# A fused attention and mixture-of-experts block: own homes for the gathered expert outputs, a new spread of the gathers, and the last expert tile's output products moved into the next unit

## The reference

```python
xn = layernorm(x)                                 # over the 128 channels
# attention: 8 heads of 32, keys and values from a latent of rank 64
q, k, v = heads(xn @ Wq.T), heads(xn @ Wkv_down.T @ Wk_up.T), heads(xn @ Wkv_down.T @ Wv_up.T)
attn = softmax(q k^T / sqrt(32)) v @ Wo.T
# experts: token -> expert floor(xn . wr + br) mod 8
ffn[token] = relu(xn W1[e] + b1[e]) @ W2[e] + b2[e]   # e = expert of the token
out = x + attn + ffn
```

## Time and profile before

| | us |
|---|---|
| median of 3 runs | 505.51 |
| lowest and highest | 501.59 and 506.85 |
| the profiled execution | 505.35 |
| its span in the trace | 503.5 |
| TensorE busy | 456.6 (91%) |
| VectorE busy | 414.5 (82%) |
| GpSimd busy | 376.5 (75%) |

### The profile page before, as it was taken

The page is one execution under the profiler, slowest core; times in us unless marked ns, Lnnn a source line. Parts: engine busy times, 40 slices in busy tenths (PEclk is TensorE's granted clock), DMA queues, the critical chain, the costliest instruction groups (busy, mean ns, idle before and its releaser), DMA issues.

```text
span 503.5 us, 15093 instructions
## 1 busy us (share of the span) xinstructions
PE 456.6 (91%) x4992; PEld 319.7 (63%) x4992; DVE 414.5 (82%) x883; ACT 346.0 (69%) x861; POOL 376.5 (75%) x399
## 2 busy tenths in 40 slices
PE   1868879999999999979999999998999989999967
PEld 1446445665656646658999999964665656656634
DVE  6998988778899899848888888875899898898865
ACT  3686457766777878847777777755766777687654
POOL 4755388888888888717777777757898888988952
PEclk9985899999999999989999999998999999999999
DMA  7994923565573896797878888726474566656322
GB/s 227 331 219 121 270 72 104 125 125 129 145 215 106 204 260 193 224 239 218 262 254 258 262 262 273 227 76 121 89 149 114 132 133 133 129 131 137 84 73 65
DMA packets 82826, 86.74 MB, mean 172 GB/s; under 512 B 10608, under 2 KB 66384, under 8 KB 82768
## 3 DMA queue, kind: packets, MB, share of 16 engines
q1 hardware_dynamic: 78672, 77.60, 57.2%
q0 software_dynamic: 4096, 8.40, 6.7%
HBM read 38.61 MB, written 22.04 MB: 120 GB/s over the span
## 4 chain that ended last, share of the span: by engine, by line
PE 43%; issue 16%; DVE 14%; POOL 13%; DMA 5%; ACT 4%; SPq 3%; POOLq 1%; ACTq 0%; DVEq 0%
POOL padd L592 12%; PE psum L1286 9%; PE psum L1251 8%; PE psum L1270 7%; DVE negm L990 6%; PE psum L1328 4%; PE psum L1301 4%; DMA stk<-mT 4%; SPq L326 3%; PE psum L1199 3%; PE psum L1200 2%; PE psum L1201 2%; DVE split L914 2%; ACT prob L724 2%; PE psum L1220 1%
## 5 line engine op out<-in xcount | busy, mean ns | idle before, releaser
L724 ACT ACTIVATE prob<-psum 128x512 f32<-128x512 f32 x256 | 150.2, 593 | 97.8 <-PE psum L1270 70.4
L990 DVE TENSOR_REDUCE negm<-psum 128x2 f16<-128x512 f32 x256 | 170.6, 682 | 43.3 <-PE psum L1251 36.2
L644 POOL TENSOR_TENSOR padd<-prob 128x512 f32<-128x512 f32 x104 | 126.6, 1218 | 34.6 <-ACT prob L724 26.3
L1251 PE MATMUL psum<-stk 96*128 96x256 f16 x512 | 101.6, 281 | 12.0 <-DVE negm L990 9.4
L592 POOL TENSOR_TENSOR padd<-xTl,padd 128x512 f16<-128x512 f32 x71 | 82.2, 1157 | 36.4 <-DVE padd L1100 36.4
L1270 PE MATMUL psum<-stk 97*128 97x256 f16 x512 | 97.8, 274 | 9.7 <-DMA stk<-mT 4.7
L794 ACT ACTIVATE xTl<-psum,xn_all 128x128 f32<-128x128 f32 x284 | 81.1, 369 | 27.5 <-POOL padd L592 20.7
L610 POOL DMA_INDIRECT xsort<-xn_all,pos x64 | 67.5, 1055 | 14.1 <-issue 13.5
L624 POOL DMA_INDIRECT xn_all<-ysort,pos x64 | 65.4, 1021 | 15.2 <-issue 7.7
L1251 PEld LDWEIGHTS psum<-stk 96*128 96x128 f16 x512 | 41.7, 98 | 54.6 <-DVE negm L990 25.8
L1286 PE MATMUL psum<-prob,vt 128*32 128x256 f32 x1024 | 70.5, 391 | 0.9 <-ACT prob L724 0.8
(11 more groups left out here) (166 smaller groups left out, 882.4 us busy)
## 6 DMA issues: line engine op xcount, KB each, us to landing
stk<-split SPq DMA_DIRECT2D x192, 128.0 KB
xn_all<-wsplit SPq DMA_DIRECT2D x71, 258.0 KB, 4.4
xsort<-oT SPq DMA_DIRECT2D x9, 512.0 KB, 4.9
xTh<-xsort SPq DMA_DIRECT2D x18, 256.0 KB, 4.0
ysort<-xTh SPq DMA_DIRECT2D x18, 256.0 KB, 4.2
out<-acc SPq DMA_DIRECT2D x15, 256.0 KB
acc<-x SPq DMA_DIRECT2D x3, 1024.0 KB, 8.4
xn_all<-W SPq DMA_DIRECT2D x12, 256.0 KB
```

What stands on the lines that cost most here:

```text
L644: nc.gpsimd.tensor_tensor(padd[:, bb, hs], prob[:, bb, hs, 0, :], prob[:, bb, hs, 1, :], ALU.add).then_inc(pool_add, 1)
L724: nc.scalar.activation(prob[:, bb, h, :, :].rearrange("p a c -> p (a c)"), bank[st_bank(u, n)], ACT.Exp, scale=SCALE).then_inc(act_exp, 1)
L990: V.tensor_reduce(negm[:, k % 2, col:col + 2], bank[n % 2].rearrange("p (a c) -> p a c", a=2), AX.X, ALU.max, negate=True).then_inc(dve_ma ...
L1251: ins = mm(bank[n % 2][:, qc * T:(qc + 1) * T], stk[0:96, s, 1, h, t0 + qc * P:t0 + (qc + 1) * P], stk[0:96, s, 0, h, t0:t0 + T], start=Tr ...
```

## The change

- Gathered chunks go to homes of their own, `xn_all[:, j, :]` for chunk j, in place of the two places of `yg`. The wait for `expert_sum(s - 2)` goes; a wait for the landing of the gathers two groups before takes its place.
- The gathers are spread anew: 2 in unit 16 (steps 6 and 7), 4 in each of units 17 to 28 (steps 1, 3, 5, 7), 5 in unit 29 (0, 1, 3, 5, 7), 5 in unit 30 (0, 2, 4, 6, 7) and 4 in unit 31 (1, 3, 5, 6). In units 30 and 31 each waits for `exp` of its step. `expert_sum` stays where it is.
- GpSimd's wait for the stores of `ysort` moves from the start of unit 16 to its step 6, behind the four additions of that unit.
- The last tile's `output(70)` moves into step 2 of unit 16, into bank 5; its `y_out(70)` to VectorE's step 3, ahead of `k_low`; `store_group(17)` into unit 16, behind `load_max(17)`. TensorE enters unit 16 after `y_out(69)`.

```diff
-                for g in range(NT // 4 - 3, NT // 4):
+                for g in range(NT // 4 - 3, NT // 4 - 1):
                     store_group(g)
...
+                    if half == 1 and first and k == 0:
+                        store_group(NT // 4 - 1)
...
-            def gather(s, i):
-                if s >= 2 and i == 0:
-                    pool.wait_ge(dve_out, s - 1)
-                j = 4 * s + i
+            def gather(j):
+
+                g = j // 4
+                if j % 4 == 0 and g >= 2:
+                    pool.wait_ge(pool_g[g % 2], 64 * (g // 2))
                 nc.gpsimd.indirect_dma_start(
-                    out=yg[:, s % 2, i, :], out_offset=None, in_=ysort,
+                    out=xn_all[:, j, :], out_offset=None, in_=ysort,
                     in_offset=bass.IndirectOffsetOnAxis(ap=pos[:, j:j + 1], axis=0)
-                ).then_inc(pool_g[s % 2], 16)
+                ).then_inc(pool_g[g % 2], 16)
+
+            def gathers_at(u):
+
+                return {NU // 2: (6, 7), NU - 3: (0, 1, 3, 5, 7), NU - 2: (0, 2, 4, 6, 7), NU - 1: (1, 3, 5, 6)}.get(u, (1, 3, 5, 7))
...
                 if u == NU // 2:
                     hidden_lows()
-                    for par in range(2):
-                        pool.wait_ge(sp_st[par], 16 * NT // 8)
...
-                    if n % 2 == 1 and u >= NU // 2:
-                        gather(u - NU // 2, n // 2)
+                    if u == NU // 2 and n == 6:
+                        for par in range(2):
+                            pool.wait_ge(sp_st[par], 16 * NT // 8)
+                    if u >= NU // 2 and n in gathers_at(u):
+                        if u >= NU - 2:
+                            pool.wait_ge(act_exp, 8 * u + n + 1)
+                        gather(fetched)
+                        fetched += 1
...
+                        if f and half == 1 and n == 3:
+                            y_out(NTC - 1, 5)
...
+                        if n == 2 and seam:
+                            output(NTC - 1, ex[NTC - 1], 5)
+                        if n == 2 and half == 1 and first and k == 1:
+                            pe.wait_ge(dve_y, NTC)
...
-            output(NTC - 1, ex[NTC - 1])
             pe.wait_ge(dve_kl, u + 3)
             pe.wait_ge(act_h32, NTC - 1)
             proj_k(u + 3, (u + 3) // 2, u + 3)
 
-            pe.wait_ge(dve_y, NTC)
+            pe.wait_ge(dve_y, NTC - 1)
```

More of the change, by code:

```diff
@@ L618, in scatters_at @@
                 return (1, 3, 5, 7) if 11 <= u < 14 else (0, 1, 3, 5, 7)
-            def gather(s, i):
-                if s >= 2 and i == 0:
-                    pool.wait_ge(dve_out, s - 1)
-                j = 4 * s + i
+            def gather(j):
+                g = j // 4
+                if j % 4 == 0 and g >= 2:
+                    pool.wait_ge(pool_g[g % 2], 64 * (g // 2))
                 nc.gpsimd.indirect_dma_start(
-                    out=yg[:, s % 2, i, :], out_offset=None, in_=ysort,
+                    out=xn_all[:, j, :], out_offset=None, in_=ysort,
                     in_offset=bass.IndirectOffsetOnAxis(ap=pos[:, j:j + 1], axis=0)
-                ).then_inc(pool_g[s % 2], 16)
-            sent = 0
+                ).then_inc(pool_g[g % 2], 16)
+            def gathers_at(u):
+                return {NU // 2: (6, 7), NU - 3: (0, 1, 3, 5, 7), NU - 2: (0, 2, 4, 6, 7), NU - 1: (1, 3, 5, 6)}.get(u, (1, 3, 5, 7))
+            sent = fetched = 0
             for u in range(NU):
@@ L1003, in last_experts @@
                 a4 = acc[:, NC - 4:NC, :]
-                V.scalar_tensor_tensor(a4, yg[:, 1, :, :], 1.0 / (WS * WS), a4, ALU.mult, ALU.add
+                V.scalar_tensor_tensor(a4, xn_all[:, NC - 4:NC, :], 1.0 / (WS * WS), a4, ALU.mult, ALU.add
                                        ).then_inc(dve_part, 1)
@@ L1035, in expert_sum @@
                 a4 = acc[:, bass.ds(s * 4, 4), :]
-                V.scalar_tensor_tensor(a4, yg[:, par, :, :], 1.0 / (WS * WS), a4, ALU.mult, ALU.add
+                V.scalar_tensor_tensor(a4, xn_all[:, bass.ds(s * 4, 4), :], 1.0 / (WS * WS), a4, ALU.mult, ALU.add
                                        ).then_inc(dve_out, 1)
@@ L1100, in hid_high, with y_out @@
                 V.tensor_copy(hh[:, t % 4, :], h32[:, t % 2, :]).then_inc(dve_hh, 1)
-            def y_out(t):
+            def y_out(t, b=None):
                 dve.wait_ge(pe_y, t + 1)
@@ L1105, in y_out @@
                     dve.wait_ge(sp_st[t // 4 % 2], t // 8 * 16)
-                V.reduce_sum(ys[:, t % 8, :], bank[2 + t % 2][:, 0:2 * D].rearrange("p (a d) -> p d a", a=2), AX.X
+                V.reduce_sum(ys[:, t % 8, :], bank[b or 2 + t % 2][:, 0:2 * D].rearrange("p (a d) -> p d a", a=2), AX.X
                              ).then_inc(dve_y, 1)
@@ L1175, in _ @@
                     y_out(t - 2)
-            for i in range(2):
-                row_max(NU // 2 + 1, LEAD - 8 + i, NU // 2 + 1)
-                y_out(NTC - 2 + i)
+            row_max(NU // 2 + 1, LEAD - 8, NU // 2 + 1)
+            y_out(NTC - 2)
+            row_max(NU // 2 + 1, LEAD - 7, NU // 2 + 1)
             body(NIT // 2, 1, True, False)
@@ L1194, in _ @@
             mm = nc.tensor.matmul
+            ex = []
             pe.wait_ge(pool_const, 4)
@@ L1395, in hidden, with output @@
                 ins.then_inc(pe_h, 1)
-            def output(t, e):
+            def output(t, e, b=None):
                 pe.wait_ge(pool_hl, t + 1)
@@ L1402, in output @@
                 k = t % 4
-                dst = bank[2 + t % 2]
+                dst = bank[b or 2 + t % 2]
                 for fc in range(FC):
@@ L1469, in _ @@
             hidden(0)
-            ex = []
             for t in range(NTC):
```

1 line of the change is left out of this document (removed).

## The result

The changed kernel takes 522.44 us in the median of 6 runs (520.31 to 526.18); beside it the kernel before took 505.31 (501.59 to 506.85). The ratio is 1.0344, with a 95% interval of 1.0313 to 1.0374: slower by 17 us. I had forecast 512.1 with a range that ended at 517.0: the sign was right, the size less than half.

A forecast was written before the change was run, and what follows sets the result against it. TensorE sets the pace, VectorE close behind; at the seam, a chain of DMA issues to the row maxima. From 505.35 us, -0.7 + 7.5 - 0.5 + 0.5 = +6.8 gave 512.1 us, range 504.5 to 517.

The forecast's parts named there:

- The seam: Ahead of unit 16: `output(70)` taken away lets units 16 and 17 start 0.72 us earlier; -0.7 us.
- the moved wait for the store: GpSimd, units 16 and 17: the wait moves to the two gathers behind the additions; costed at nothing.
- When the gathers are issued and land: Units 17 to 28: step-3 gather starts 2.1 us before `expert_sum`; last packet 2.9 us after start in the mean, semaphore 0.45 more.
- From lateness to loss: Units 17 to 28: late sums, less room, cost TensorE 2.7 us in odd and 4.8 in even units; +7.5 us.
- The rooms of the even units: Even units 18 to 28: late `row_max` loses 0.8 us in unit 22; 1.4, 0, 0.6, 0.6, 1.4 in the others.
- That losses add up: Units 17 to 28: late TensorE delays the next `exp`, addition and gather by as much, so losses sum; together +7.5 us.
- Unit 29 and the end: Unit 29: TensorE's 0.58 us idle for `row_max` goes, -0.5 us; unit 31: last gather later, end +0.5 us.
- All gathers land in time: Rival, units 17 to 28: every gather as quick as unit 17's; 506.0 us, or 504.6 if covered; chance 0.24.
- The clock: Rival: unit 16's added work avoids the clock fall at 348 to 352 us, worth 1.7 us; 502.9 us; chance 0.08.
- The stalls feed on themselves: Rival: TensorE's stalls bring clock falls of 1.7 us each; from three on, over 517 us; chance 0.08.
- The rival that the seam gives nothing: Unit 16: the product in step 2 pushes `scores_T` behind it; +0.7 us on any case; chance 0.1, inside the others.

The follow-up runs named there:

- product_alone: Kernel before with only the last tile's product, sum, store and GpSimd's store wait moved; old homes, four gathers in unit 16: 506.66 us, ratio 1.0034.
- spread_alone: Kernel before with own homes and the new gather spread, the last tile's product, sum and store left in place: 516.35 us, ratio 1.0318.
- hold_odd: Kernel before with two short VectorE reductions ahead of `expert_sum` in odd units only of 17 to 28: 506.68 us, ratio 1.0064.
- catch_up: Changed kernel with its two missing gathers made good in units 17 and 18 (five each) instead of at the end: 502.36 us, ratio 1.0034.
- hold_both: Kernel before with short VectorE reductions ahead of `expert_sum` in units 17 to 28, two in odd and four in even units: 514.43 us, ratio 1.0198.
- even_three: Kernel before with three short VectorE reductions ahead of `expert_sum` in even units 18 to 28, none in odd: 506.0 us, ratio 1.0107.
- homes_alone: Kernel before with own homes and the wait on earlier gathers instead of `expert_sum(s - 2)`; slots and product old: 509.38 us, ratio 1.009.
- one_in_16: Changed kernel with one gather in unit 16 instead of two, each group's last gather one slot later: 549.89 us in a single run, ratio 1.09.
- four_in_16: Changed kernel with four gathers in unit 16, each group complete one unit before its sum: 504.56 us, ratio 0.9984.

## Why the prediction was wrong, step by step

- **The seam, -0.7 us.** In the traces it came: from the start of the last `scores` behind `output(69)` to `proj_k` it takes 0.22 us (337.38 to 337.60), before 0.95. Another 0.9 us, which I had not forecast, came on top: from `exp` of unit 16 to unit 17's first `scores_T` it takes 8.90 us, before 9.79, and the row maxima landed 3.9 us after their issue where the earlier trace rows have 4.75. All five kernels with both the moved product and the own homes have it, neither product_alone (9.88) nor spread_alone (9.84); why, no run shows. TensorE's row there:

```profile
347.57 0.39 PE L1283 MATMUL psum<-stk 97*128 97x256 f16 x2 [0.70 <-DMA stk<-mT]
```

  In the medians it is not to be seen: 1.0344 with the product moved, 1.0318 without. That the moved wait for the store costs nothing did not hold: at full clock unit 17 lasts 11.90 us from `q_high` to `q_high` in the changed kernel, 10.40 in hold_odd. The fall of the clock that the kernel before has in that unit, worth 1.6 to 1.7 us, hid it. (catch_up, on the other chip, has the same two gathers there and 10.40 us too; it pays behind that, with the 2.82 us above.)
- **When the gathers are issued and land.** Right, in part by luck. The slots were those of the kernel before, and from the last gather's start to the start of the sum it takes 3.32 us in the mean of the twelve (2.54 to 4.62); I had worked out 2.9 + 0.45 = 3.35. But the last packet ends 2.7 us after that start in the mean, and from there to the sum it is 0.6 (0.4 to 0.9), so two errors cancel. That SyncE's traffic holds the late packets up was argued; no run tests it. An estimate from the Trainium skill's figure, 2.15 us ("DMA: Bandwidth & Descriptors", Anatomy of one DMA — SWDGE (gpsimd) path), counted from the end of the 0.96 us instruction, makes 3.1, where 3.32 were measured in the mean; of the spread of 2 us it says nothing.
- **From lateness to loss: the step that failed.** The prediction's sums have 6.1 of the 7.5 us in units 17 to 27; 11.3 were lost there. Put the measured starts of the sums into the same sums and they still give 6.1: neither the gathers nor the rooms make the difference. What does is this:
  - *The length of the sum, 0.68 us.* It is recorded with 0.99 in the mean, since moved back it runs into GpSimd's short addition. So sums end 1.48 us late in the mean, not 1.20. With the measured ends the same sums give 8.1, so this term was 2.0 us too small.
  - *A late unit costs its lateness less its room, and nothing else.* Each of the five even units lost 0.43 us more, 2.2 together, at the place told under hold_both. I had put that at nothing; its cause is open.
  - The remaining 1.0 us lies in the odd units: 1.5 in units 19 to 27, less the 0.5 by which unit 17 reads shorter. Some 0.4 of it is their room, 0.9 by hold_odd where I had 1.0. The rest I can give to nothing.
- **The rooms of the even units.** Right, unit by unit. The prediction shows `scores` of unit 22 at 409.45, whose room of 1.25 us is the wait of 1.21 for `stk<-mT` just ahead of it, but the losses that it gives for the other five (1.4, 0, 0.6, 0.6, 1.4) come out only with each unit's own room, 0.06 to 0.2 in units 18, 24, 26 and 28 and 0.7 in unit 20. It doesn't say so, and a reader who takes the room of unit 22 for that of all gets 1.2 us for the six. even_three bears the rooms out.
- **That losses add up.** They do, but for the 0.43: by the holds, 2.0 us in odd units and 3.9 in even ones, with 2.2 for the latter, make the 8.2 of hold_both.
- **Unit 29 and the end.** TensorE's idle 0.58 us of the earlier trace rows is gone, as said. But -0.5 and +0.5 us were forecast together, and +2.2 us came behind unit 28's gather, of which 1.4 are forecast for unit 28's own late sum (TensorE stands idle 2.08 us for it). GpSimd's gathers at 494.79, 496.31 and 497.56 us run back to back, and ScalarE then stands idle 2.46 us to 499.12: the signature of homes_alone in small. The clock fell for 3.4 us at 483.8, which is 1.7 us. The kernel before that I summed against had a disturbed end itself, which I had not seen as such: 38.3 us, where kernels with paced gathers and nothing late need 34 to 37. The last `normalise` came late as said, and more so: the last projection shows 1.43 us of idle time for it in place of 0.39.
- **The rivals.** "All gathers land in time" fell: none of twelve did. "The clock" fell: the fall of the earlier trace rows did go, but another came at 483.8. "The stalls feed on themselves" had the right side, over 517 us, and a mechanism that is real: not in the changed kernel's profiled execution, where no fall is recorded in units 17 to 28, but twice in these units of spread_alone and nine times in one_in_16, behind late `row_max`. How much of the changed kernel's median it makes, only the mean clocks of the six executions say: some 3 us at most. I gave it 0.08. The rival that the seam gives nothing is right for the medians.

The profiled execution lies 8.2 us over the forecast: 5.2 in units 17 to 27, as above; 2.2 ahead of them, where the first half's shifts make 2.5, which have nothing to do with the change; and 0.8 behind unit 28's gather. The median lies another 2.1 us above the profiled execution, for which the clock is the candidate. Shown by experiment is that the slot of the last gather makes the loss; how the loss divides among these terms is read from single traces.

## What to carry to other kernels

When an operation is made late, price three things: its room in every unit that it stands in (a room that is another transfer's wait, as in unit 22, is there in some units only), its own length at the new place, where it may run into another engine's work (0.99 us here for 0.68), and the clock, which may fall behind the new idle times. A transfer that is issued for the step which uses it should be judged by the slowest of its kind, not by the mean; here one slot earlier cost nothing that can be measured, and this slot 3%. A backlog is best made good in the first units, since each further one pays for it again. And before two ratios are set against each other, see on which chip each was measured.

## What the runs showed of the hardware beyond that

- On one chip, indirect gathers of 64 KB sent back to back, one each 1.25 us, go with idle times of 2 to 4 us in TensorE, VectorE or ScalarE, which wait for none of them (homes_alone, four_in_16, product_alone, the kernel before). On the other chip eight in a row go without them (even_three).
- Between the gathers of units 17 and 28 TensorE is idle 28 of 151.5 us in one_in_16, and the granted clock falls there to 0.5 for 3.4 us nine times, each worth 1.6 us. In the changed kernel's profiled execution it is idle 10.8 of 122.2 us, and the clock does not fall.
- Two, three and four VectorE reductions of 0.6 us ahead of a sum all end it 4.06 us behind the gather, where the sum or the reductions meet GpSimd's short addition: 1.26 us for the sum in place of 0.68, 1.21 for the addition in place of 0.73.
- A sum that waits for a gather can start 2.5 to 4.6 us after that gather did, for the same 64 KB in the same place of the unit; the step from the last packet to the sum is 0.4 to 0.9 us of it.
